# Neighbour tables as one stream of slots, with border steps shared and masked, and TensorE adding the weighted rows of the last attention

## The reference, cut to what matters

```python
def _L3_gnn_ref(x, edge_index, W, att_src, att_dst, bias):      # 8 heads of 32
    h = jnp.einsum('nf,fhd->nhd', x, W)
    a_src = jnp.sum(h * att_src, axis=-1)
    a_dst = jnp.sum(h * att_dst, axis=-1)
    e = jax.nn.leaky_relu(a_src[src] + a_dst[dst], NEG_SLOPE)
    e_max = jax.ops.segment_max(e, dst, num_segments=N)
    e_exp = jnp.exp(e - e_max[dst])
    denom = jax.ops.segment_sum(e_exp, dst, num_segments=N)
    alpha = e_exp / (denom[dst] + 1e-16)
    out = jax.ops.segment_sum(h[src] * alpha[:, :, None], dst, num_segments=N)
    return jax.nn.relu(out.reshape(N, -1) + bias)
```

## Time and profile before

| | us |
|---|---|
| median of 3 runs | 5052.19 (5048.85 to 5056.97) |
| profiled execution | 5050.65 |
| its span, first to last instruction | 5049.0 |
| PE, DVE, ACT, POOL busy | 2837.1, 3175.9, 1613.8, 2036.4 |
| last stage (l3a) | 3663 to the end |
| gate attention beside experts (l1a) | 2116 to about 2632 |

### The profile page before, as it was taken

How to read it: one execution, slowest core, us unless ns; L and a number is a source line. 1 busy time by engine, 2 the same in 40 slices (tenths; PEclk the granted TensorE clock), 3 DMA queues, 4 the chain that set the end, 5 groups by cost and what they waited for, 6 DMA issues and landing times. The chain is left out here.

```text
span 5049.0 us, 66259 instructions
## 1 busy us (share of the span) xinstructions
PE 2837.1 (56%) x15435; PEld 2098.0 (42%) x15474; DVE 3175.9 (63%) x7737; ACT 1613.8 (32%) x2880; POOL 2036.4 (40%) x1967
## 2 busy tenths in 40 slices
PE   0541055699799596467761699859400133344447
PEld 0431055587687485355551244447300122222224
DVE  8886687677577656334436754452456777777774
ACT  0243043476476121144430454322201222222222
POOL 1136410200100152577761100016377777777771
PEclk9999999899899598588885899979755566667679
DMA  0412345542442323211114554522343333333220
GB/s 33 77 20 45 17 167 196 170 139 83 166 140 83 116 65 115 91 30 35 35 38 132 196 174 161 172 91 67 101 117 91 90 90 85 93 95 84 77 63 19
DMA packets 341260, 487.28 MB, mean 97 GB/s; under 512 B 171624, under 2 KB 259056, under 8 KB 339059
## 3 DMA queue, kind: packets, MB, share of 16 engines
q1 hardware_dynamic: 204434, 259.76, 16.5%
q0 software_dynamic: 86064, 176.05, 13.2%
q10 hardware_dynamic: 50608, 49.90, 3.0%
HBM read 369.96 MB, written 137.24 MB: 100 GB/s over the span
## 5 line engine op out<-in xcount | busy, mean ns | idle before, releaser
L2355 POOL DMA_INDIRECT l3a_got<-rows,l3a_idx x896 | 949.4, 1060 | 304.1 <-issue 273.6
L2449 PE MATMUL ps<-l3a_xt,l3a_w 128*128 128x512 f32 (+1 forms) x448 | 266.9, 759 | 633.1 <-ACT l3a_h L2393 633.1
L1662 PE MATMUL ps<-l0a_all_rows,l0a_w 128*128 128x257 f32 x2500 | 556.8, 382 | 28.3 <-DVE l0a_w L1782 28.3
L1662 PEld LDWEIGHTS ps<-l0a_all_rows,l0a_w 128*128 128x128 f32 x2500 | 476.0, 191 | 101.9 <-issue 32.0
L2757 POOL DMA_INDIRECT l1a_got<-rows,l1a_idx x384 | 383.6, 999 | 131.3 <-issue 127.4
L2449 PEld LDWEIGHTS ps<-l3a_xt,l3a_w 128*128 128x128 f32 x448 | 112.3, 277 | 766.9 <-issue 766.6
L2077 PE MATMUL ps<-l2a_table,l2a_count 128*128 128x512 bf16 x1837 | 404.8, 380 | 40.5 <-ACT l2a_count L2002 38.6
L2379 ACT ACT_TABLE_LOAD x99 | 127.0, 1283 | 772.0 <-DVEq L2519 772.0
L2780 PE MATMUL ps<-xt,l1w_w 128*128 x640 | 208.0, 485 | 156.5 <-ACT l1a_h L2836 111.4
L2077 PEld LDWEIGHTS ps<-l2a_table,l2a_count 128*128 128x128 bf16 x1875 | 183.4, 98 | 262.1 <-issue 43.2
L1587 ACT ACTIVATE l0a_low<-ps,l0a_factors x650 | 254.6, 510 | 85.7 <-PE ps L1652 78.2
(11 more groups left out here) (995 smaller groups left out, 6622.9 us busy)
## 6 DMA issues: line engine op xcount, KB each, us to landing
l0a_held<-counts SPq DMA_DIRECT2D x130, 640.0 KB, 3.9
counts<-count_held SPq DMA_DIRECT2D x13, 3200.0 KB, 9.9
l2a_held<-counts SPq DMA_DIRECT2D x65, 640.0 KB, 4.0
l3a_got<-rows,l3a_idx POOLq DMA_INDIRECT x896, 2.8
l_y<-l1a_y_sb ACTq DMA_DIRECT2D x20, 640.0 KB, 3.4
l2a_table<-rows SPq DMA_DIRECT2D x16, 640.0 KB, 7.5
l2a_state<-l1a_fresh ACTq DMA_DIRECT2D x1, 9984.0 KB
l2a_seen<-l2a_state POOLq DMA_DIRECT2D x12, 768.0 KB, 5.9
```

Of the source, the lines that this page charges most:

```text
L1662: ins = pe.matmul(sums_of(n, k, D + 1), w[:, at, k * P:(k + 1) * P], all_rows[:, at, 1:RW], start=(at == 0), stop=False)
L2355: pool.indirect_dma_start(out=got[:, at:at + RW], out_offset=None, in_=rows[:, :], in_offset=bass.IndirectOffsetOnAxis(ap=idx[:, a, k:k + ...
L2449: ins = pe.matmul(ps[:, m, 0:size * P], w1[:, x, k, m * P:(m + 1) * P], xt[:, 0:size, k, :], start=(k == 0), stop=(k == KT - 1))
```

## The change

1. **Tables.** Both tables become arrays (P, columns). Each tile takes as many columns as its largest in-degree (at least FEWEST = 8), and the next begins right behind it, wherever that falls in an octet. `write_tile` becomes `write_table`: the whole octets of each tile are written first; then, when all are stored, one closing octet per tile, read so that it ends at the tile's last slot. `fill` computes where, in some ten more operations on one partition; `steps_of` is gone. Unused slots hold c.N.
2. **A row for nobody.** `rows` has N + 1 rows; the last one holds zeros and scores of FLOOR, written by an SP DMA ahead of the gathers, for which POOL waits (`blank_in`). It is fetched like any other.
3. **Steps.** In l1a and l3a a step is always a whole octet. An octet on the border of two tiles is gathered once and worked on in a step of both; `mask_of` adds FLOOR to the scores of slots that aren't the tile's. The reset of the ring's scores, and the filling of the ring at the start, go. A ring place is freed (`freed`) at the start of the next step. In l1a the half steps go, and the tile's registers are loaded from two table values (`Stream.bounds`).
4. **Sums.** In l3a TensorE adds the 8 weighted rows of a step by eight products with the identity into one PSUM bank, and DVE adds that bank to the accumulator after the weighted rows of the next step (`summed`); `rows_v` has two places. The tree is gone.
5. `count_neighbours` reads its index columns as one slice of the table; the score rows of l2a are preset with FLOOR.

The diff, cut:

```diff
-        def write_tile(eng, s, t, stored):
+        def write_table(eng, s, odd, emptied=None):
+
+            eng.wait_ge(s.sized, 1)
...
+                        with eng.Fori(0, n_units) as u:
+                            eng.dma_start(s.table[:, bass.ds(to + u * SLOTS, SLOTS)],
+                                          s.ell[:, bass.ds(t, 1), bass.ds(SLOTS + u * SLOTS, SLOTS)].rearrange("p o s -> p (o s)")).then_inc(s.stored, 16)
+                done = eng.value_load(s.wrote_i[0:1, 0:1], min_val=1, max_val=s.chunks * NT * s.whole_row)
+                when(eng, c, s.stored, done * 16)
+                with eng.Fori(0, (NT + 1 - odd) // 2) as h:
+                    t = h * 2 + odd
+                    at = eng.value_load(s.last_i[0:1, 0, bass.ds(t, 1)], min_val=1, max_val=WIDE)
+                    to = eng.value_load(s.last_i[0:1, 1, bass.ds(t, 1)], min_val=0, max_val=s.columns - WIDE)
+                    eng.dma_start(s.table[:, bass.ds(to, SLOTS)],
+                                  s.ell[:, bass.ds(t, 1), bass.ds(at, SLOTS)].rearrange("p o s -> p (o s)")).then_inc(s.closed, 16)
...
-                odd_tiles(m)
+                write_table(act, m, 1)
                 act.wait_ge(g.told, 1)
                 with nc.allow_non_contiguous_dma(reason="one word per node"):
                     act.dma_start(ranks[:, 0].rearrange("(t p) -> p t", p=P), g.rank_i[:, :]).then_inc(ranks_in, 16)
-                odd_tiles(g)
+                write_table(act, g, 1)
...
+    def rounds(self, total):
+        return (total + RING * SLOTS) // (RING * SLOTS)
...
+def mask_of(masks, row, H):
+    return masks[:, :, :, :].rearrange("p k r j -> p (k r j)")[:, bass.ds(row * SLOTS, SLOTS)].unsqueeze(2).broadcast_to([P, SLOTS, H])
...
+                def sums(t, o):
+                    when(pe, c, valued, o + t + 1)
+                    rows_now = weighed_rows(o)
+                    for k in range(ADDED):
+                        ins = pe.matmul(totals, c.ident[:, :], rows_now[:, k, :, :].rearrange("p h d -> p (h d)"),
+                                        start=(k == 0), stop=(k == ADDED - 1))
+                    ins.then_inc(summed, 1)
+
+                def tile(t, begins, ends, at):
+                    sums(t, begins // SLOTS)
                     at(0)
+                    with pe.Fori(begins // SLOTS + 1, ends // SLOTS + 1) as o:
+                        sums(t, o)
                     at(1)
...
+                    if not opening:
+                        add_sums(o + t)
+                        ch(dve.tensor_tensor(acc[:, :, :], acc[:, :, :], spread(p[:, SLOTS, :], DH + 1), ALU.mult))
+                    dve.sem_inc(valued, 1)
+
+                def add_sums(done):
+
+                    when(dve, c, summed, done)
+                    ch(dve.tensor_tensor(acc[:, :, :], by_head(totals), acc[:, :, :], ALU.add))
```

412 lines of the change are left out of this document (195 added, 217 removed).

## The result

The changed kernel takes **5170.02 us** (median of 4 runs, 5163.07 to 5173.69) beside 5053.5 for the kernel before on the same chip: ratio 1.023, interval 1.0212 to 1.0247. The prediction said 5019, with a range of 4975 to 5085. It had the wrong sign, and the time lies outside the range.

The account below looks back on a forecast made before the run. In l3a, POOL's gathers were taken to bound tiles 0 to 11 and DVE the later ones. Terms l3a −11, l1a −22, table building +1, counting −1 sum to −33: 5017.6 profiled, about 5019 us, range 4975 to 5085.

Parts of the forecast that it names:

- TensorE's sum: l3a: eight identity matmuls take 3.7 us at full clock, 5.5 after a pause, both hidden in a loop step; 7.3 isn't.
- w: l3a, each tile's end: DVE's wait for TensorE's last sum, 0 to 4 us, taken as 1.2.
- E: Rival, l3a: all sums at the lower clock, 7.3 us against 6.4, +176, giving 5195; chance 0.04.
- F: Rival: ACT's table switch takes 1.4 us longer behind gelus, twice per tile in 20 tiles, 56 us, giving 5075; chance 0.04.
- C: Rival, l3a: sums stand behind expert halves on TensorE; 3.7 us uncovered per tile in 20 tiles, giving 5093; chance 0.13.
- B: Rival: a warmer TensorE hides everything; l3a −30, l1a −35, giving 4986; chance 0.17.
- The loop step: DVE in l3a: 8.16 − 3.14 (tree) + 1.68 (exponential) + 0.6 (add, rescaling) + 0.16 (mask) = 7.46 us; bounds 7.1 to 8.2.
- By tiles: l3a: tile 0 nothing, tiles 1 to 4 −11, 5 to 11 −16, 12 to 24 +16; together −11, bounds −35 to +25.
- the other condition for its failure: l3a: the forecast would be wrong if ring slots freed a step later made POOL wait in tiles 1 to 11.
- Table building: Building both tables: fewer writes, but closers wait for all earlier writes; between −9 and +10 us, taken as +1.
- The step on the ranks' write: Table building: this write moves back some 22 us, out of the gate entries' gather, so DVE gets that up to 9 us sooner.
- l1a: First attention: −25 in tiles 0 to 11, −5 in 12 to 24, +8 at the end; −22 us, bounds −5 and −40.

Follow-up runs that it names:

- e5: The changed kernel with DVE's add tree back in l3a in place of TensorE's sums, stream and masks kept; 5534.1 us, 1.0203 against the kernel before.
- e12: The kernel before, with its old tables and 112 steps, with only TensorE's sums in place of the tree in l3a; 5680.1 us, ratio 1.0493.
- e4: The changed kernel with both values of each table write packed into one, so one register load instead of two; 5651.6 us, 1.0419 against the kernel before.

## Why the prediction was wrong, point by point

- **TensorE's sum: right.** 3.7 and 5.5 us were forecast; the rows have 3.72 and 5.51. It hides in loop steps (0.24 of idling, for DVE's own product). w was taken as 1.2 us per tile end, about 30 in all; the 25 tile ends have 46.1, 1.8 each. E (all sums at 1.2 GHz; the prediction calls it the last rival, but F is) and F (a dearer table switch: 1.66 us of waiting) didn't come. C came in part at most: 3.7 us or more were waited in 6 tiles and not in 20, and the expert adds wait 55.6 us for outputs (12 times), hardly more than the 52.8 (11 times) of before. B's condition came, a warmer TensorE (0.79 to 0.88), without B's gain.
- **The loop step: the failed term.** Forecast 7.46, measured 8.46. Three parts of it: the mask, taken as 0.16 with a bound of 0.3, costs 0.72 up to the copy of the maxima (2.04 against 1.32), since the register arithmetic for its row stands between it and the scores, 0.60 of idling in each of 101 loop steps, and since L2515, which it replaces, had overlapped the next operation (L2516 began 0.11 us behind it); the exposed exponential 1.83 for 1.68 (5034.48 to 5036.31); product, add, rescaling and the way round the loop 4.59 for the 3.70 before, where 0.6 more was forecast. 0.56 + 0.15 + 0.29 = 1.00. Over 101 loop steps that is 101 us, and l3a missed its forecast of −11 by just 101 (+90). That the two agree so closely is partly luck: by tiles the misses are 8, 9, 28 and 55 us, where the steps alone would give 6, 20, 30 and 45. The prediction priced the mask as an operation, by its data, from rows in which no register arithmetic of DVE's stood at that place.
- **By tiles.** Tile 0: 0 forecast, +8. Tiles 1 to 4: −11, measured −2.2. Tiles 5 to 11: −16, measured +12.3; their 30 loop steps times 1.0 are about the difference (the forecast's −9 there also counts 34 old loop steps where there are 27; with 27 it is −4). Tiles 12 to 24: +16, measured +71; 45 loop steps and some 10 us more, of tile ends above all. The forecast that the gathers' pace stays under 1.38 was right, and the other condition for its failure came: in tiles 1 to 11, where POOL had never waited for DVE, it now waits 91 us, and 280 in all of l3a. So DVE sets the pace of these tiles, too.
- **Which part of the change?** The prediction had one step for stream and sums together, 0.66 shorter than before. e5 takes them apart: the stream costs 1.33 per loop step and 14 more steps, the sums give back 1.03 (0.5 on the old tables, e12).
- **Table building: +18, forecast +1 (−9 to +10).** The step on the ranks' write was right: DVE's part ended 9 us sooner. Missing was the term for the closers: they were counted (25 each) and said to wait for earlier writes, but their own serial time, 13 on SP's queue by 2.05 us, was priced nowhere, nor that the next stage waits for them. e4 shows the loads in it: 16 us for one of two.
- **l1a: −9.3, forecast −22.** Register loads were sized right: idling ahead of the first scores is 2.4 (2.44 and 1.83 in late tiles). Tiles 0 to 10 went from 270.6 to 256.1, by 14.5, where the forecast took 25 off tiles 0 to 11. POOL still sets the pace there, with no wait for DVE of over 0.5 us, but by tile 11's begin it has issued 200 gathers instead of 212, and so 12 fewer, where 19 fewer were reckoned. In the later tiles POOL waits 37.8 us for DVE, and the time up to DVE's last store is only 4 shorter (5 forecast for tiles 12 to 24). The end cost 10 (8 forecast), through SP's queue and surplus gathers.
- **The other chips.** That the same change costs 4.6% on some chips, no view of the trace before could show. There TensorE's sums account for 129 of the 260 us by which l3a is longer, with 357 us in which DVE idles behind sums that had ended, and the prediction has no term for that.

## What to carry to other kernels

An operand whose place is computed at run time is priced by the register arithmetic that the engine's sequencer must do between the operation before and this one (0.49 us and 0.60 of idling here, 0.11 and 0.20 where one record does it), not by its elements: look for a row with such an operand, multiply the idling ahead of it by the loop's count before looking at the data saved, and keep the arithmetic out of the loop where it isn't needed. Work that is taken off one engine and handed to a second puts a signal in series with the loop, and what was a cover for another wait (here the tree for the exponential) has to be counted twice, once as work that goes and once as the wait that comes out. Short serial writes with loaded addresses at a stage's end (2 us each here) are a stage of their own.
